# Moving TensorE's register load of the expert number from the up-projection to the down-projection in a routed feed-forward and Mamba kernel

## The reference

```
x = x + 0.5 * ffn(layernorm(x))      # 8 experts, the best 2 per token, hidden size 512
x = x + mixer(layernorm(x))          # two Mamba blocks, the second followed by a chunked memory read
x = x + 0.5 * ffn(layernorm(x))      # the same 8 experts again

# ffn, for each expert e:
h   = silu(xf @ w1s[e])                        # up-projection, 128 -> 512
out = out + combine[:, e:e+1] * (h @ w2s[e])   # down-projection, 512 -> 128
```

## Time and profile before

| | |
|---|---|
| median of 3 runs | 1761.77 us (1754.93 to 1763.77) |
| the profiled execution's own time | 1761.77 us |
| its span, first to last instruction | 1759.7 us |
| TensorE matmul busy (PE) | 1298.2 us, 74% |
| TensorE weight load busy (PEld) | 1163.6 us, 66% |
| VectorE busy (DVE) | 1365.4 us, 78% |
| ScalarE busy (ACT) | 1264.4 us, 72% |
| GpSimd busy (POOL) | 603.9 us, 34% |
| mean granted TensorE clock | 0.877 of full speed |

### The profile page before, as it was taken

How to read it: one execution, slowest core, us unless ns; L and a number is a source line. 1 busy time by engine, 2 the same in 40 slices (tenths; PEclk the granted TensorE clock), 3 DMA queues, 4 the chain that set the end, 5 groups by cost and what they waited for, 6 DMA issues and landing times. The chain is left out here.

```text
span 1759.7 us, 29139 instructions
## 1 busy us (share of the span) xinstructions
PE 1298.2 (74%) x8528; PEld 1163.6 (66%) x8528; DVE 1365.4 (78%) x2144; ACT 1264.4 (72%) x2641; POOL 603.9 (34%) x639
## 2 busy tenths in 40 slices
PE   2837756887888788887878788878888786578435
PEld 2727755776767677776767677767777685567335
DVE  1228798899789898888889888989898989887500
ACT  1229766897779787887889787979788787478212
POOL 2221424134251626154333525162515413321311
PEclk9858966998999899898999899989999898689757
DMA  6525644667576757676676757676767674557323
GB/s 211 144 58 111 134 78 106 142 146 160 128 169 149 177 132 171 139 162 134 138 174 151 165 132 177 148 162 141 168 136 159 139 150 92 111 126 151 69 77 94
DMA packets 153383, 242.49 MB, mean 138 GB/s; under 512 B 14480, under 2 KB 87952, under 8 KB 153104
## 3 DMA queue, kind: packets, MB, share of 16 engines
q0 software_dynamic: 40448, 134.25, 39.5%
q1 hardware_dynamic: 112784, 106.38, 21.0%
HBM read 94.95 MB, written 28.18 MB: 70 GB/s over the span
## 5 line engine op out<-in xcount | busy, mean ns | idle before, releaser
L1347 POOL DMA_DIRECT2D acc<-G x224 | 204.6, 913 | 878.0 <-DMA acc<-G 418.2
L812 ACT ACTIVATE dA<-delta,A 128x255 f32<-128x255 f32 x1024 | 425.7, 495 | 4.4 <-DVE hs L1127 3.4
L444 PE MATMUL b_h<-xsT,wst 128*128 128x128 f32 x1920 | 287.0, 297 | 39.8 <-issue 24.5
L1133 DVE TENSOR_TENSOR_SCAN hs<-dA,b_r 128x512 f32<-128x512 f32 x256 | 298.0, 1202 | 17.5 <-PE b_r L548 10.2
L1127 DVE TENSOR_TENSOR_SCAN hs<-dA,dbu 128x1024 f32<-128x1024 f32 x128 | 292.7, 2287 | 14.7 <-ACT dA L812 8.2
L1146 DVE TENSOR_TENSOR G<-hs,b_r 128x1024 f32<-128x1024 f32 x224 | 272.3, 1215 | 39.8 <-PE b_r L559 28.1
L444 PEld LDWEIGHTS b_h<-xsT,wst 128*128 128x128 f32 x1920 | 257.5, 208 | 60.2 <-issue 56.9
L453 PE MATMUL b_out<-w2s,hT 128*128 x1920 | 269.4, 287 | 11.6 <-ACT ys L742 7.3
L453 PEld LDWEIGHTS b_out<-w2s,hT 128*128 128x128 f32 x1920 | 247.1, 201 | 17.4 <-issue 15.2
L708 ACT ACT_TABLE_LOAD x180 | 230.9, 1283 | 3.9 <-PEq L1480 0.7
L750 ACT ACTIVATE hT<-b_h 128x512 f32<-128x512 f32 x240 | 139.6, 595 | 120.5 <-PE b_h L444 119.1
(11 more groups left out here) (155 smaller groups left out, 1736.8 us busy)
## 6 DMA issues: line engine op xcount, KB each, us to landing
acc<-G POOLq DMA_DIRECT2D x224, 512.0 KB
wst<-w_dram SPq DMA_DIRECT2D x240, 256.0 KB, 3.0
xsort<-sorted SPq DMA_DIRECT2D x80, 192.0 KB, 5.2
results<-ys SPq DMA_DIRECT2D x80, 192.0 KB, 3.2
xin<-x_dram SPq DMA_DIRECT2D x8, 256.0 KB, 4.9
sorted<-xn,posi POOLq DMA_INDIRECT x128
yk<-results,posi POOLq DMA_INDIRECT x128
out_dram<-ob SPq DMA_DIRECT2D x8, 256.0 KB, 2.6
```

The lines of the kernel that those rows point to most:

```text
L444: last = mm(H[r % 2][:, w], wst[k % NW][:, w], xsT[i // CH % 2][:, t:t + P], start=True, stop=True)
L812: last = do(dA[j % 4][:, d, k, 1:], delta[b][:, k, 1:], ACT.Exp, scale=A[:, k, s:s + 1])
L1133: V.tensor_tensor_scan(hs[j % 2][:, d, :, :].rearrange("p h t -> p (h t)"), dA[j % 4][:, d, :, :].rearrange("p h t -> p (h t)"), R[u % 2][ ...
L1347: Q.dma_start(acc[b][:, :, :, :].rearrange("p d h t -> p (d h t)"), G[j % NG][:, :, :, :].rearrange("p d h t -> p (d h t)"), accum_op=ALU. ...
```

## The change

The load of the expert number into TensorE's register is taken out of `ffn_up` and put into `ffn_down`, behind that function's waits. The dictionary that carried the register from one to the other is gone.

```diff
-            owners = {}
-
             def ffn_up(n, i):
-                owners[i] = pe.value_load(eid[n % 2][0:1, i:i + 1], min_val=0, max_val=E - 1)
                 r, k, t = RING_OF["U", i], n * NT + i, i % CH * P
                 pe.wait_ge(s_w[k % NW], 16 * (k // NW + 1))
                 wait(pe, f_hact, n * ITEMS + max(r - 1, RING_OF["T", i // CH] + 1))
...
                 pe.wait_ge(f_hact, n * ITEMS + RING_OF["U", i] + 1)
                 if i % CH == 0:
                     wait(pe, f_ys, n * CHUNKS + i // CH)
-                e = owners.pop(i)
+                e = pe.value_load(eid[n % 2][0:1, i:i + 1], min_val=0, max_val=E - 1)
                 for c in range(HC):
                     last = mm(Y[:, i % CH * D:(i % CH + 1) * D], hT[i % NH][:, c, :], w2s[:, e, c, :],
                               start=c == 0, stop=c == HC - 1)
```

## The result

| | |
|---|---|
| before, median of 14 runs | 1760.64 us (1754.40 to 1769.06) |
| changed, median of 14 runs | 1782.76 us (1767.53 to 1793.55) |
| ratio | 1.0118, 95% interval 1.0093 to 1.0144 |
| profiled execution, before / changed | 1761.77 / 1785.28 us, spans 1759.7 / 1783.4 |

In microseconds 1.18% is 21, where I had forecast +5 and given slower by over 0.5% a chance of 0.30. The time lies outside my range. The granted clock does not explain it: it was 0.877 and 0.866 in the two profiled executions, but the median over the changed kernel's runs is 0.873, and that of the kernel before was 0.870 to 0.873 in the measurements beside the experiments.

A forecast was written before the change was run, and what follows sets the result against it. VectorE was taken as nearest to a bound in the interleaved part, with a third of TensorE's delays on the path. Last pass 2.2, first 1.3 and middle 1.3 us made +4.8: 1766 us, range 1752 to 1779.

The forecast's parts named there:

- The ends: First and last pass, nothing running beside the feed-forward work: delays count in full, +1.3 us and +2.2 us.
- What was removed: Sequencer idling ahead of up-projections in the fourteen middle passes: 24 to 52 us of TensorE's time, 38 taken.
- What was added: Idling ahead of down-projections in the fourteen middle passes: 42 us of TensorE's time, a third on the path.
- 126 x 0.39 x 0.65 = 32 us are lost at the D: Middle passes: 126 down-projections first behind a mixer step, 39% caught as at up-projections, 0.65 us each.
- 16 x 0.65 = 10: Middle passes: down-projections that showed a wait for ScalarE, 8 for the copy and 8 for the silu, 10 us.
- the lead of D1: Last pass: sequencer 0.85 us ahead of the array, enough to hide the load at down-projections behind an up-projection or turning.
- How much each: Load price at a down-projection where the sequencer has just come out of a wait: 0.65 us.
- What share is on the path: Middle passes: one third of a TensorE delay counts, as 73.5 of VectorE's 222.7 us idling ended with TensorE.
- The slower one: Down-projections at group heads caught nearly always: 92 us added, 24 removed, about 1788 us; chance 0.25.
- The faster one: Up-projection gains reach the path, down-projection losses don't: 52 us removed, 10 added, 1751 us; chance 0.15.
- The passing sequencer: Sequencer passes a waiting matmul, so only up-projections behind a down-projection give anything back: 1771 us; chance 0.05.
- both places are free: Rival of no effect: both load places lie under waits that are there anyway, 1762 us; chance 0.10.

The follow-up runs named there:

- e11: Kernel before with the change made in the first and last pass alone, the 14 interleaved passes as before: ratio 1.0020 to the kernel before.
- e1: Kernel before with a second load behind the waits of each down-projection, the up-projection's load kept but unused, 480 loads: ratio 1.0183 to the kernel before.
- e4: Changed kernel with the load in the down-projection put ahead of both its waits: ratio 1.0023 to the kernel before.
- e2: Kernel before with one load per pass; every down-projection takes the first tile's slice of `w2s`, so outputs are wrong: ratio 0.9947 to the kernel before.
- e3: Kernel before with the load moved behind the four matmuls of each up-projection: ratio 0.9974 to the kernel before.
- e12: Repeat of e3, load behind the up-projection's matmuls, against the kernel before: ratio 0.9966.

## Why the prediction was wrong

**The ends** were right. In the last pass four D and the last one took their load late, each about 0.64 us, and the four gaps ahead of U closed. The other D kept their places. By the starts of the weight loads and of the last copy the pass grew from 33.6 (1706.14 to 1739.78) to 37.4 us (1726.00 to 1763.38), 3.7 and not 2.2. The rest, 1.4 us between U1 and D1, is the clock: in the changed kernel it was granted at 0.50 of full speed from 1730.4 to 1733.7, and in the kernel before it rose to full at that place, with a mean of 0.72 from 1710.5 to 1711.6 and 1.00 from there to 1713.4. Why it rose later is not known; TensorE had idled 24.8 us ahead of the pass and 25.5 before. The first pass grew by 0.9 us, where I had 1.3, and e11 measured 3.5 us for both ends, which was the forecast, though its interval is wide. D0 took 1.83 us for eight weight loads in the changed kernel,

```profile
1732.04 1.83 PEld L450 LDWEIGHTS b_out<-w2s,hT 128*128 128x128 f32 x8
```

and 0.97 before.

```profile
1711.67 0.97 PEld L453 LDWEIGHTS b_out<-w2s,hT 128*128 128x128 f32 x8
```

**What was removed** was right too. I had 38 us of TensorE's time in the middle and one third of it, 12.7 us, and 1.7 in the ends. Measured were 51.9 - 9.1 = 42.8 us of issue and, by e1 against the changed kernel, 11 us (4 to 19) for middle and ends together. The share was nearer to a fifth, though a third is not excluded.

**What was added is the step that failed**, the term "126 x 0.39 x 0.65 = 32 us are lost at the D" with "16 x 0.65 = 10" for ScalarE's waits, 65 D in all. I had 42 us of TensorE's time and 14 us on the path. Measured by the same rows are 79.2 - 14.2 = 65 us, and by e1, less the 5.2 us that the ends have without their gaps, 27 us (21 to 33). Taken apart:

- How many: 98 D, not 65. This is the term that was mis-sized. Going through the fourteen passes in the two traces D by D (a D counts as caught when TensorE's weight loads idle over 0.15 us ahead of it; that gives 18 and 101, since the passes reach a little beyond the windows), of the 126 that stand first in a group 11 were caught before and 69 now, where I had 49 more. Of the 84 others 7 were caught before and 32 now, and for these I had only those that already showed a wait. I counted as waiting for ScalarE only the D ahead of which the array stood idle. A wait that ends while the array still works on the piece ahead leaves no idle row, but it takes the sequencer's lead. The 25 newly caught inside a group show it: for 21 of them the load began within 0.15 us of the end of the silu or copy that they wait for. Of the 58 newly caught at the head of a group 26 began within 0.25 us of it. Of all 69 caught there 50 stand behind a "t" or a "k" step, as the D3 above does.
- Why the lead of D1 misled me. I took 0.85 us from D1 of the last pass as the sequencer's lead, and took every D behind a U for covered by it. But its silu ended at 1711.98 + 0.60 = 1712.58, and its first register instruction ran at 1712.6:

```profile
1711.98 0.60 ACT L750 ACTIVATE hT<-b_h 128x512 f32<-128x512 f32 x1 [1.05 <-PE b_h L444]
```

So the 0.85 us were the time from its release by ScalarE to its turn on the array, and they hold only where ScalarE is as prompt. In the middle passes it has the mixer's work too, busy 1199.8 of 1520 us. With that fits e4, whose load stands ahead of both waits and which is 0.95% faster than the changed kernel.
- How much each: right, partly by luck. 65 us over 98 D is 0.66, where I took 0.65. The load itself was longer than I took it for: the median is 308 ns in the changed kernel, but 99 of its 240 loads took over 330 ns and the mean is 493. This one, ahead of D6 of an early pass, took about three times the median:

```profile
L448 PEldq TENSOR_LOAD <-eid x1: 898/898/898, 175.6 to 175.6; - x1
```

The longest of the earlier trace rows, 1447 ns, should have made me ask for the spread. What made up for it is that many of the newly caught D still had a part of the lead: they idled 0.62 us on average and 0.49 at the median.
- What share is on the path. I took one third everywhere, from VectorE's waits for TensorE. At D it is 27 / 65 = 0.42 (0.33 to 0.50), at U a fifth. So the exchange of 43 us at U for 65 at D is worse than its net of 22 us: with the same share for both, at most 9 us would follow. Why a delay at D weighs more than one at U is not shown. VectorE's wait for "k" grows in the changed kernel and not in e4, which points to that step but doesn't prove it.

Of the 16 us by which 4.8 fell short of 21, the number of D makes (65 - 42) / 3 = 8, the share at D 5 and the smaller give-back 3.

**The rivals.** The slower one named the place and its test, "issue" ahead of D over 70 us in the middle, which came out at 79.2. But 14.2 of that was there before, and its mechanism holds only in part: 69 of the 126 heads were caught, not nearly all, and 32 of the 101 D that were caught stood inside the groups. Its price of 92 added and 24 removed was wrong in both terms (65 and 43), and its sum of 1788 us is close to 1783 by luck: one third of its net of 68 us makes 23, and the measured net of 22 us cost about 17, nearly all of itself. The faster one is excluded: D's results are not wanted at once, but what is queued behind D is. The passing sequencer was not tried further, and its 1771 us lie below the interval; the earlier trace rows remain the evidence against it: in the 25.5 us of that wait no load ran. That both places are free is excluded by e1 and e2.

## What to carry to other kernels

On TensorE a register load from SBUF held up what stood behind it in the queue: D3 of the last pass started 0.88 us behind its release with the load and 0.24 without it. In this kernel its price on the array was what the sequencer lacked in lead, 65 us over the 98 D that idled. So put it behind the last instruction of a group, as behind the four matmuls of U, and ahead of whatever waits next (e3: 43.1 us of issue where before had 72.1, ratio 0.9974), not between a wait and the work that the wait releases: the same 256 loads cost 0.2% ahead of a wait, within the noise of nothing, and 1.2% behind it. And when such an instruction is moved behind a wait, count every wait whose release comes within its length of the array's own end, not only those that show idle time: 98 D idled here, and only 16 had shown a wait for ScalarE before. A lead read off one place may be only the distance to the last release there, as the 0.85 us of D1 were. Before two "issue" rows are compared, look at which instruction carries the wait: with register instructions in between, D's idling stood under "issue" (15.2 us before), and with most of them gone under ScalarE (16.2 us, and 3.0 under "issue", in e2).

## What the runs showed of the hardware that was not expected

- A TENSOR_LOAD of one number took 296 to 1447 ns with a median of 306 and a mean of 484; 65 of the 240 took over 600 ns, and so did 69 of 240 in the changed kernel. In both, single ones of some 900 ns stand beside ones of 300. What makes them long wasn't tried.
- TensorE's idling cost far less than its length, 0.2 to 0.4 us of time for each us. U (0.2) and "t" (0.2) lie below D in e1 (0.4); "k" (0.3) can't be told from either.
- The first pass differs by more than the effects studied here. From its first turning to the start of its last copy it took 46 us in the profiled execution of the kernel before and 51.5 us in that of e3. Most of it is one wait: ahead of D9, 4.75 us, for a copy that ScalarE itself began late, released by something that the profile doesn't name:

```profile
37.23 0.88 PE L432 MATMUL b_h<-prm,xsort 128*128 128x128 f32 x3 [16.84 <-DMA xsort<-sorted]
...
76.19 0.49 ACT L742 ACTIVATE ys<-b_out 128x384 f32<-128x384 f32 x1 [2.39 <-remote]
...
76.92 1.78 PEld L453 LDWEIGHTS b_out<-w2s,hT 128*128 128x128 f32 x8 [4.75 <-issue]
...
88.74 0.49 ACT L742 ACTIVATE ys<-b_out 128x384 f32<-128x384 f32 x1 [1.33 <-PE b_out L453]
```

From 76.5 to 81.5 the clock of e3 was granted at 0.50 of full speed, where the kernel before had it in full (1.00) from 73 to 80. e12, the same kernel as e3, shows the same wait (4.84 us) and 52.8 us. Such a wait of 2.8 to 5.5 us ahead of a D in the first pass stands in the D rows of every experiment and in neither of the two kernels' own profiles; without it the share of e3 is 0.15 and the others move by under 0.05. So spans of single executions don't tell a change of 0.3% in this kernel; the ratios of many runs do.
